# Image tower on one core: GpSimd's bulk work in the layers moved to the patch stage, ScalarE and PE

## The chip, the core and the metric

One Trainium2 chip, one of its cores. The metric is the device time of one launch in microseconds, median over runs. The engines are PE (TensorE, matmuls; its clock is granted at 1.2 or 2.4 GHz, shown as 0.50 and 1.00), VectorE (DVE), ScalarE (ACT), GpSimd (POOL) and SyncE (SP), which here issues every DMA. Everything is float32.

## What is computed

64 images of 84 x 84 pixels go through a tokenizer (patches of 14 x 14, windows of 3 x 3 patches with an attention inside each, one attention over the four windows of an image), which gives 6 tokens of 256 channels per image, 384 in all. Then come four residual steps, each after a layer norm:

```python
h = concat(cls_tok, L0_tok(x))
h = h + L0_attn(layernorm(h))   # gated scan along the tokens, then W_o and b_o
h = h + L0_ffn(layernorm(h))    # weight quantized to -1, 0, 1 times a scale
h = h + L1_attn(layernorm(h))   # 16 heads; output o_w and o_b
h = h + L1_ffn(layernorm(h))    # 8 experts, each with its top 48 tokens
```

Inside them, where the change touches them:

```python
# L0_attn(x): out = h_scan @ W_o.T + b_o
return x + out
# L1_attn: the head matrices
core_sym = 0.5 * (core + core.T)
centered = head_residual - head_residual.mean(axis=0, keepdims=True)
head_mats = core_sym[None] / float(H) + centered
...
y = y @ o_w.T + o_b
# L1_ffn(x): the normed tokens are a residual too
out = xf.at[flat_idx].add(o.reshape(k * n, d))
```

So the first and the fourth residual step add the normed tokens as well: h + norm(h) + product.

## The kernel before

The program is written engine by engine, each engine's queue in order, with semaphores between them. Three stages follow each other.

The patch stage has 19 tiles of 126 patches. For each, SP loads a tile into one of three buffers (L291), PE convolves it (L372), ScalarE copies it out (L1390), VectorE sums the windows (L870), takes statistics (L857, L879) and norms it (L864), GpSimd computes the reciprocal root of the variance (L1579, L1581) and keeps a copy of the normed tile (L1585), PE turns it. A norm of tile t - 1 stands behind the statistics of tile t. SP then loads the layer weights, with the head matrices at their end, in one DMA (L312). The window attention and the global attention follow.

In the layers the tokens lie as four tiles of 96 rows by 256 channels, in two groups (images 0 to 31 and 32 to 63) of two tiles. One norm is: VectorE's statistics (L1139, L1142), the reciprocal root on GpSimd (`rs_tokens`, L1569 and L1571, two small instructions), VectorE's norm of two tiles (L1153). PE turns the normed tiles (L644), ScalarE copies them (L1493), PE multiplies (`channels` L651, `tokens` L660).
GpSimd also does bulk work in the layers, in this order in its queue: behind the roots of the first norm, for each group, base = h + xn (L1648) and base + b_o (L1650); then the head matrices, 16 of 64 x 64, in nine instructions (L1664 to L1673), on which PE waits at L702; roots of the second norm; a memset (L1682); roots of the third norm; base = h + o_b (L1685); roots of the fourth and fifth norm; a memset (L1691); base = h + xn (L1695); the weighted picks (L1699). VectorE waits for `base_ready` before the first residual (L1203), the second norm (L1150), the third residual (L1289) and the output (L1375).

VectorE's gated scan: keep and gate from the tanh (L1183, L1184), gate times value (L1191), scan (L1194), for one group after the other, then the ternary weights (L1198 to L1201), then the first residual. In the last layer VectorE picks the top tokens in six rounds (L1312, L1317), with the fifth norm's two groups between them, while PE does 24 keep-warm matmuls (L749); the gather is L761.

## Time and profile before

| | us |
|---|---|
| median of 3 runs | 280.37 |
| lowest, highest | 278.83, 283.74 |
| the profiled execution | 281.46 |
| its span, first to last instruction | 279.7 |
| PE busy | 252.7 |
| VectorE busy | 154.4 |
| ScalarE busy | 66.8 |
| GpSimd busy | 67.9 |

The views of the trace are read like this. A time line has the start in us from the span's begin, the duration, the engine, the line, the operation, output and inputs with their shapes, and in brackets how long the engine was idle before and what ended it; rows of one line may be merged (x2: two instructions, from the start of the first to the end of the last). The chain of waits goes back from the last instruction to what released it, and is printed in order of time. A window row has the stretch, its length, the busy time and number of records for PE, PE's weight load, VectorE, ScalarE and GpSimd, the mean granted PE clock, the busy share of the DMA engines and GB/s. A group has the line, engine, operation and form with its count, then busy us, the mean in ns, and the idle time before.

### The profile page before, as it was taken

What the parts mean: (1) busy time and instruction counts of PE and PEld (TensorE: products, weight loads), DVE (VectorE), ACT (ScalarE), POOL (GpSimd) and SP (SyncE); (2) the same over time, 40 slices, a digit from 0 to 9 for tenths busy, and PEclk for the clock granted to TensorE, in tenths of its full rate; (3) what the DMA queues carried; (4) which work ended last, traced back from release to release, by engine and by line L of the source; (5) the groups of instructions that cost most, each with busy time, mean ns of one, the idle gap of its engine ahead of it and who ended that gap; (6) DMA issues with size and microseconds to landing.
All of it is one profiled execution on the core that took longest, in us unless ns stands there. A gap on an engine that the chain in (4) does not pass through costs nothing.

```text
span 279.7 us, 4102 instructions
## 1 busy us (share of the span) xinstructions
PE 252.7 (90%) x1467; PEld 194.5 (70%) x1467; DVE 154.4 (55%) x392; ACT 66.8 (24%) x166; POOL 67.9 (24%) x130
## 2 busy tenths in 40 slices
PE   6999999998999899789579899979989599999994
PEld 4888888975798677677457799856558454555562
DVE  1476767567685554459947444554358962621212
ACT  1134424235754422113010340000000003301200
POOL 0254434330222210199334100001017060000000
PEclk9999999999999887689989995555579979999999
DMA  6567754999400047980000000000000000676002
GB/s 196 160 223 225 223 177 117 415 404 428 187 1 2 0 111 243 425 348 2 0 1 0 2 0 2 0 0 0 0 0 4 1 0 0 231 294 227 2 0 56
DMA packets 8626, 32.94 MB, mean 118 GB/s; under 512 B 1056, under 2 KB 2848, under 8 KB 6432
## 3 DMA queue, kind: packets, MB, share of 16 engines
q1 hardware_dynamic: 8608, 32.70, 32.6%
q8 instruction: 11, 0.18, 0.3%
q14 instruction: 7, 0.06, 0.1%
HBM read 32.30 MB, written 0.39 MB: 117 GB/s over the span
## 4 chain that ended last, share of the span: by engine, by line
PE 70%; DVE 19%; issue 3%; ACT 2%; POOL 2%; DMA 1%; SPq 1%; DVEq 0%; POOLq 0%
PE bank L372 15%; PE bank L816 5%; PE bank L790 5%; PE bank L660 5%; DVE desk L1153 3%; PE bank L731 3%; PE bank L362 3%; PE bank L538 3%; PE bank L716 3%; PE bank L824 3%; PE bank L761 3%; PE bank L516 2%; PE bank L492 2%; PE bank L651 2%; PE bank L708 2%
## 5 line engine op out<-in xcount | busy, mean ns | idle before, releaser
L372 PE MATMUL bank<-desk,attic 118*126 118x256 f32 x190 | 43.9, 379 | 1.4 <-DMA desk<-conv_w 1.4
L362 PE MATMUL bank<-zeros 128*128 128x256 f32 x142 | 41.6, 442 | 1.1 <-POOL small L1562 1.1
L372 PEld LDWEIGHTS bank<-desk,attic 118*126 118x126 f32 x190 | 34.4, 188 | 6.2 <-DMA desk<-conv_w 1.8
L362 PEld LDWEIGHTS bank<-zeros 128*128 128x128 f32 x142 | 30.0, 221 | 7.0 <-issue 1.2
L1569 POOL TENSOR_SCALAR small<-small 96x2 f32<-96x2 f32 (+2 forms) x15 | 3.4, 226 | 87.5 <-DVE small L1142 77.7
L660 PE MATMUL bank<-layw,desk 128*96 128x256 f32 x48 | 16.7, 514 | 5.7 <-DVE desk L1194 3.6
L1493 ACT ACTIVATE desk<-bank 128x384 f32<-128x384 f32 x8 | 3.9, 491 | 62.3 <-PE bank L644 62.3
L660 PEld LDWEIGHTS bank<-layw,desk 128*96 128x96 f32 x48 | 10.1, 221 | 11.4 <-DVE desk L1194 4.2
L857 DVE BATCH_NORM_STATS2 small<-desk 126x6 f32<-126x256 f32 x19 | 8.1, 426 | 17.2 <-ACT desk L1390 17.1
L870 DVE TENSOR_REDUCE window_sums<-attic 118x70 f32<-118x630 f32 (+1 forms) x19 | 14.8, 784 | 4.3 <-DMA attic<-patches 3.8
L1390 ACT ACTIVATE desk<-bank 126x256 f32<-126x256 f32 x19 | 7.3, 384 | 40.3 <-PE bank L372 40.3
L1153 DVE TENSOR_SCALAR desk<-desk,small 96x256 f32<-96x256 f32 x20 | 13.4, 708 | 3.4 <-POOL small L1571 3.2
L1395 ACT ACTIVATE attic<-bank,cols 128x126 f32<-128x126 f32 (+1 forms) x38 | 14.9, 455 | 0.0
L731 PEld LDWEIGHTS bank<-desk,cons 48*128 48x128 f32 x48 | 11.4, 325 | 4.0 <-issue 2.7
L651 PE MATMUL bank<-desk,layw 128*128 128x192 f32 x72 | 13.3, 345 | 0.6 <-ACT desk L1493 0.6
L731 PE MATMUL bank<-desk,cons 48*128 48x32 f32 (+5 forms) x48 | 13.6, 455 | 0.0
L651 PEld LDWEIGHTS bank<-desk,layw 128*128 128x128 f32 x72 | 12.8, 205 | 0.9 <-ACT desk L1493 0.8
L1262 DVE TENSOR_TENSOR desk<-bank,desk 128x64 f32<-128x64 f32 (+5 forms) x12 | 4.7, 395 | 15.8 <-PE bank L731 12.5
L1579 POOL TENSOR_TENSOR small<-small 126x1 f32<-126x1 f32 x19 | 3.7, 193 | 37.6 <-DVE small L879 37.6
L516 PE MATMUL bank<-desk,attic 126*128 126x112 f32 (+1 forms) x76 | 10.5, 280 | 1.3 <-ACT attic L1438 0.7
L1346 DVE TENSOR_TENSOR desk<-bank,attic 128x512 f32<-128x512 f32 x8 | 5.5, 692 | 10.7 <-PE bank L790 10.7
L816 PE MATMUL bank<-resident_experts,desk 128*64 128x256 f32 x80 | 11.0, 382 | 0.5 <-DVE desk L1353 0.5
(189 smaller groups left out, 458.9 us busy)
## 6 DMA issues: line engine op xcount, KB each, us to landing
resident_experts<-experts SPq DMA_DIRECT2D x10, 1024.0 KB, 14.8
attic<-experts SPq DMA_DIRECT2D x6, 1024.0 KB, 10.3
attic<-patches SPq DMA_DIRECT2D x19, 315.0 KB, 2.9
layw<-layer_w SPq DMA_DIRECT2D x1, 2760.0 KB, 11.8
desk<-tokenizer_w SPq DMA_DIRECT2D x4, 576.0 KB, 4.5
attic<-bias SPq DMA_DIRECT2D x8, 256.0 KB, 4.5
cons<-constants SPq DMA_DIRECT2D x1, 692.0 KB, 5.5
desk<-conv_w SPq DMA_DIRECT2D x5, 128.0 KB, 3.1
```

The source lines that it names most:

```text
L362: mm(bank[b][:, 0:C], zeros[:, 0:P], zeros[:, :], start=True, stop=True)
L372: i = mm(conv_bank[j][0:TP, 0:C], xt[j][0:KP, k, :], convw[0:KP, k, :], start=(k == 0), stop=(k == KX - 1))
L516: i = mm(bank[4 + k][:, u * H8 * WT:u * H8 * WT + H8 * n], xhat_all[0:n * NWIN, t, k * P:(k + 1) * P], s_attT[q % RING][0:n * NWIN, u, 0:H ...
L538: i = mm(bank[b][:, m * width:(m + 1) * width], w_[:, k, m * P:(m + 1) * P], src[:, k, w * width:(w + 1) * width], start=(k == 0), stop=(k ...
L651: i = mm(bank[b][:, at:at + GT], w[:, k, cols_:cols_ + P], src[:, k, :], start=(k == 0), stop=(k == KC - 1))
L660: i = mm(bank[b][0:TR, u * C:(u + 1) * C], srcT[:, k, u * TR:(u + 1) * TR], w[:, k, :], start=(k == 0), stop=(k == KC - 1))
L731: i = mm(bank[4 * g + 1 + t % 3][:, p * GT:p * GT + GI * (t + 1)], spread[:, t, :], att[0][:, g * GI:(g + 1) * GI, p, 0:t + 1], start=True ...
L790: i = mm(bank[c][side * SW:(side + 1) * SW, :], ysT[:, k, e, :], w1[:, k, c * 512:(c + 1) * 512], start=(k == 0), stop=(k == KC - 1))
L816: i = mm(bank[4][side * SW:(side + 1) * SW, 0:C], hidT[q % 2][:, f, side * SW:(side + 1) * SW], w2[:, f, :], start=(f == 0), stop=(f == FC ...
L870: dve.tensor_reduce(sums[0:KP][:, bass.ds(t * (KX * WT), KX * WT)], xt[j][0:KP].rearrange("p k (w n) -> p (k w) n", n=NWIN), AX.X, ALU.add)\
L1153: ts(dst[0:TR, t, :], src[0:TR, t, :], t_mv[0:TR, t, 0:1], t_rs[0:TR, t:t + 1], ALU.subtract, ALU.mult).then_inc(s("xn_ready"), 1)
L1395: i = ac(winT[:, k, bass.ds(t * TP, TP)], tr_bank[j][:, k * P:k * P + TP], ACT.Identity, bias=col("kv_b", k), scale=col("kv_g", k))
```

## The change

- The weights of the heads move to the front of the packed layer weights and are loaded by a DMA of their own (64 rows, 4.5 KB each) behind the third patch tile's. The head matrices are made by GpSimd in the patch stage, one to three instructions in each of the tiles 3 to 12, in 13 instructions; the mean and the symmetric core are joined first, so one addition over four heads at a time is left. `tree` moves from the window sums to the token buffer h0T. GpSimd's loop over tiles 6 to 11 is written out.
- Residual plus norm is made by ScalarE for the first and the fourth norm, as h * (1 + r) - m * r with r the reciprocal root and m the mean: one activation for each tile (`with_norm`). GpSimd computes the two columns with three small instructions (`rs_and_shift`), one of them ahead of the root.
- The output biases b_o and o_b are put into the PSUM banks by PE, as a row of ones times the bias row (`bias_row`, two matmuls with one contraction row for each group), ahead of the token products. These take the place of `keep_warm(7, 3)` and `keep_warm(3, 1)`. The third residual then adds to h itself.
- Semaphores around the class query (`c_turned`, `c_q_done`, `c_qk_done`, `c_ln`, `c_qbd`) are joined into two. The waits stay where they were.

```diff
-LAYW, LAYW_N = offsets([("w_in", KC * 2 * C), ("w_s", KC * C), ("w_o", KC * C), ("tern", KC * C),
+LAYW, LAYW_N = offsets([("heads", NH * R), ("core", R), ("coreT", R), ("w_in", KC * 2 * C), ("w_s", KC * C), ("w_o", KC * C), ("tern", KC * C),
                         ("basis", KC * 2 * R), ("v_w", KC * C), ("o_w", KC * C), ("gate", KC * E8),
-                        ("heads", NH * R), ("core", R), ("coreT", R), ("bo_row", C), ("ob_row", C)])
+                        ("bo_row", C), ("ob_row", C)])
+HEADS_N = NH * R + 2 * R
...
+        tree = h0T[0:R].rearrange("p k i t -> p (k i t)")[:, 0:NH // 2 * R].rearrange("p (h r) -> p h r", r=R)
...
+        t_up, t_nm, t_dn, ones = tiny(TT), tiny(TT), tiny(TT), tiny(P, parts=1)
...
+            sp.dma_start(layw[0:R, 0:HEADS_N], layw_d[0:R, 0:HEADS_N]).then_inc(s("heads_in"), 16)
...
-            sp.dma_start(layw[:, :], layw_d).then_inc(s("layw_in"), 16)
+            sp.dma_start(layw[:, HEADS_N:], layw_d[:, HEADS_N:]).then_inc(s("layw_in"), 16)
...
-            def tokens(b, srcT, w, done):
+            def bias_row(b, name):
+
+                for u in range(TG):
+                    mm(bank[b][0:TR, u * C:(u + 1) * C], ones[0:1, 0:TR], w_of(layw, LAYW, name, parts=1),
+                       start=(u == 0), stop=False, skip_group_check=True)
+
+            def tokens(b, srcT, w, done, biased=False):
                 for u in range(TG):
                     for k in range(KC):
                         i = mm(bank[b][0:TR, u * C:(u + 1) * C], srcT[:, k, u * TR:(u + 1) * TR], w[:, k, :],
-                               start=(k == 0), stop=(k == KC - 1))
+                               start=(k == 0 and not biased), stop=(k == KC - 1), skip_group_check=biased)
...
-            keep_warm(7, 3)
+            pe.wait_ge(s("constants_set"), 4)
+            for g in groups:
+                bias_row(4 * g + 1, "bo_row")
             for g in groups:
                 pe.wait_ge(s("scan_ready"), g + 1)
-                tokens(4 * g + 1, scanT[:, g], lw["w_o"], "mix_done")
+                tokens(4 * g + 1, scanT[:, g], lw["w_o"], "mix_done", biased=True)
...
-            pe.wait_ge(s("heads_ready"), 1)
+            pe.wait_ge(s("heads_ready"), 4)
...
+                    bias_row(0, "ob_row")
                     pe.wait_ge(s("y_ready"), T - 1)
-                    tokens(0, yT[:, 0], lw["o_w"], "lat_out_done")
-            keep_warm(3, 1)
+                    tokens(0, yT[:, 0], lw["o_w"], "lat_out_done", biased=True)
+            bias_row(4, "ob_row")
             pe.wait_ge(s("y_ready"), (T - 1) * G)
-            tokens(4, yT[:, 1], lw["o_w"], "lat_out_done")
+            tokens(4, yT[:, 1], lw["o_w"], "lat_out_done", biased=True)
...
+                if n == 4:
+                    dve.wait_ge(s("shift_ready"), G + g + 1)
...
-                if n == 1:
-                    dve.wait_ge(s("base_ready"), g + 1)
...
-                dve.wait_ge(s("base_ready"), G + g + 1)
-                add_to_h(g, 4 * g, base, "lat_out_done", g + 1)
+                add_to_h(g, 4 * g, h, "lat_out_done", g + 1)
...
+            def with_norm(i, g):
+
+                act.wait_ge(s("up_ready"), G * i + g + 1)
+                act.wait_ge(s("shift_ready"), G * i + g + 1)
+                if i:
+                    act.wait_ge(s("h_ready"), 2 * G + g + 1)
+                for u in range(TG):
+                    t = TG * g + u
+                    n = ac(base[0:TR, t, :], h[0:TR, t, :], ACT.Identity, bias=t_dn[0:TR, t:t + 1],
+                           scale=t_up[0:TR, t:t + 1])
+                n.then_inc(s("base_ready"), 1)
+
+            for g in groups:
+                with_norm(0, g)
...
+                with_norm(1, g)
...
+            core = w_of(layw, LAYW, "core", parts=R)
+            coreT = w_of(layw, LAYW, "coreT", parts=R)
+            n_head = 0
+
+            def head_step(i):
+
+                nonlocal n_head
+                n_head += 1
+                i.then_inc(s("head_steps"), 1)
+                pool.wait_ge(s("head_steps"), n_head)
+
+            def prepare_heads(t):
+
+                if t == 3:
+                    pool.wait_ge(s("heads_in"), 16)
+                    head_step(pool.tensor_tensor(core, core, coreT, ALU.add))
+                    head_step(pool.tensor_scalar(core, core, 0.5 / NH, None, ALU.mult))
+                if t in (4, 5):
+                    a = 4 * (t - 4)
+                    head_step(pool.tensor_tensor(tree[:, a:a + 4, :], heads[:, a:a + 4, :], heads[:, a + 8:a + 12, :], ALU.add))
+                if t in (6, 7, 8):
+                    n = (4, 2, 1)[t - 6]
+                    head_step(pool.tensor_tensor(tree[:, 0:n, :], tree[:, 0:n, :], tree[:, n:2 * n, :], ALU.add))
+                if t == 8:
+                    head_step(pool.tensor_scalar(tree[:, 0, :], tree[:, 0, :], 1.0 / NH, None, ALU.mult))
+                    head_step(pool.tensor_tensor(core, core, tree[:, 0, :], ALU.subtract))
+                if 9 <= t < 13:
+                    four = heads[:, 4 * (t - 9):4 * (t - 8), :]
+                    pool.tensor_tensor(four, four, core.unsqueeze(1).to_broadcast([R, 4, R]), ALU.add)\
+                        .then_inc(s("heads_ready"), 1)
...
-            for t in range(HEAD):
+            for t in range(MID):
                 rs_tile(t, t % RING)
                 if t:
                     keep_xhat(t - 1, (t - 1) % RING)
                 if t == 3:
                     pool.wait_ge(s("c_norm"), 2)
                     rsqrt(c_ve[0:1], c_mv[0:1, 1:2], c_rs[0:1], "c_rs_ready", parts=1)
-            with pool.Fori(HEAD // RING, MID // RING) as r:
-                for j in range(RING):
-                    rs_tile(RING * r + j, j)
-                    keep_xhat(RING * r + (j - 1), (j - 1) % RING)
+                prepare_heads(t)
...
-            bo = w_of(layw, LAYW, "bo_row")[0:TR].unsqueeze(1).to_broadcast([TR, TG, C])
-            ob = w_of(layw, LAYW, "ob_row")[0:TR].unsqueeze(1).to_broadcast([TR, TG, C])
             groups = range(G)
-            part = lambda v, g: v[0:TR, TG * g:TG * (g + 1), :]
-
-            for g in groups:
-                rs_tokens(0, g)
-            for g in groups:
-                pool.wait_ge(s("xn_ready"), TG * (g + 1))
-                pool.wait_ge(s("h0_ready"), g + 1)
-                pool.tensor_tensor(part(base, g), part(h, g), part(xn, g), ALU.add).then_inc(s("base_step"), 1)
-                pool.wait_ge(s("base_step"), g + 1)
-                pool.tensor_tensor(part(base, g), part(base, g), bo, ALU.add).then_inc(s("base_ready"), 1)
-
-
-            pool.wait_ge(s("layw_in"), 16)
-            core = w_of(layw, LAYW, "core", parts=R)
-            coreT = w_of(layw, LAYW, "coreT", parts=R)
-            nh = 1
-
-            def hstep(i):
-                nonlocal nh
-                nh += 1
-                i.then_inc(s("head_steps"), 1)
-                pool.wait_ge(s("head_steps"), nh)
-
-            pool.tensor_tensor(core, core, coreT, ALU.add).then_inc(s("head_steps"), 1)
-            hstep(pool.tensor_tensor(tree, heads[:, 0:NH // 2, :], heads[:, NH // 2:NH, :], ALU.add))
-            n = NH // 4
-            while n:
-                hstep(pool.tensor_tensor(tree[:, 0:n, :], tree[:, 0:n, :], tree[:, n:2 * n, :], ALU.add))
-                n //= 2
-            hstep(pool.tensor_scalar(core, core, 0.5 / NH, None, ALU.mult))
-            hstep(pool.tensor_scalar(tree[:, 0, :], tree[:, 0, :], 1.0 / NH, None, ALU.mult))
-            hstep(pool.tensor_tensor(heads, heads, tree[:, 0:1, :].to_broadcast([R, NH, R]), ALU.subtract))
-            pool.tensor_tensor(heads, heads, core.unsqueeze(1).to_broadcast([R, NH, R]), ALU.add)\
-                .then_inc(s("heads_ready"), 1)
+
+            def rs_and_shift(n, g, i):
+
+                sl = slice(TG * g, TG * (g + 1))
+                pool.wait_ge(s("t_mv_ready"), TT * n + TG * (g + 1))
+                if i:
+                    pool.wait_ge(s("base_ready"), G)
+                pool.tensor_scalar(t_nm[0:TR, sl], t_mv[0:TR, sl, 0], -1.0, None, ALU.mult).then_inc(s("nm_ready"), 1)
+                rs_tokens(n, g)
+                pool.wait_ge(s("t_rs_ready"), G * n + g + 1)
+                pool.wait_ge(s("nm_ready"), G * i + g + 1)
+                pool.tensor_scalar(t_up[0:TR, sl], t_rs[0:TR, sl], 1.0, None, ALU.add).then_inc(s("up_ready"), 1)
+                pool.tensor_tensor(t_dn[0:TR, sl], t_nm[0:TR, sl], t_rs[0:TR, sl], ALU.mult)\
+                    .then_inc(s("shift_ready"), 1)
+
+            for g in groups:
+                rs_and_shift(0, g, 0)
...
-                pool.wait_ge(s("h_ready"), G + g + 1)
-                pool.tensor_tensor(part(base, g), part(h, g), ob, ALU.add).then_inc(s("base_ready"), 1)
-            for n in (3, 4):
-                for g in groups:
-                    rs_tokens(n, g)
+                rs_and_shift(3, g, 1)
+            for g in groups:
+                rs_tokens(4, g)
...
-            for g in groups:
-                pool.wait_ge(s("h_ready"), 2 * G + g + 1)
-                pool.wait_ge(s("xn_ready"), 3 * TT + TG * (g + 1))
-                pool.tensor_tensor(part(base, g), part(h, g), part(xn, g), ALU.add).then_inc(s("base_ready"), 1)
```

## Rows read from the trace of the kernel before

**Rows 1.** The page, busy time of each engine: us, share of span, instructions.
```profile
PE 252.7 (90%) x1467; PEld 194.5 (70%) x1467; DVE 154.4 (55%) x392; ACT 66.8 (24%) x166; POOL 67.9 (24%) x130
```

**Rows 2.** The chain of waits, 112 to 170 us: start, us, what.
```profile
119.89 2.69 DVE desk L1153 x2
...
130.19 2.65 DVE desk L1191
...
132.87 2.98 DVE desk L1194
...
138.99 0.68 DVE desk L1160
...
152.37 2.64 DVE desk L1153 x2
...
155.05 0.55 PE bank L644 x4
```

**Rows 3.** Time line of GpSimd (POOL) in the layers: start, us, instruction.
```profile
129.59 2.82 POOL L1672 TENSOR_TENSOR layw<-layw,window_sums 64x1024 f32<-64x1024 f32 x1
132.50 2.53 POOL L1673 TENSOR_TENSOR layw<-layw 64x1024 f32<-64x1024 f32 x1
...
152.30 2.54 POOL L1685 TENSOR_TENSOR desk<-desk,layw 96x512 f32<-96x512 f32 x2
...
212.16 2.64 POOL L1695 TENSOR_TENSOR desk<-desk 96x512 f32<-96x512 f32 x2
```

**Rows 4.** Time line of VectorE (DVE), same shapes, and norms at 212.91.
```profile
128.73 0.56 DVE L1191 TENSOR_TENSOR desk<-desk 128x384 f32<-128x384 f32 x1
129.32 0.96 DVE L1194 TENSOR_TENSOR_SCAN desk<-desk 128x384 f32<-128x384 f32 x1
...
207.62 0.73 DVE L1153 TENSOR_SCALAR desk<-desk,small 96x256 f32<-96x256 f32 x2 [1.13 <-POOL small L1571]
...
212.91 2.04 DVE L1153 TENSOR_SCALAR desk<-desk,small 96x256 f32<-96x256 f32 x2
```

**Rows 5.** Time line of PE; in brackets the idle time before.
```profile
118.29 3.75 PE L651 MATMUL bank<-desk,layw 128*128 128x192 f32 x16
...
123.76 5.47 PE L651 MATMUL bank<-desk,layw 128*128 128x192 f32 x32 [0.58 <-ACT desk L1493]
...
130.36 1.95 PE L660 MATMUL bank<-layw,desk 128*96 128x256 f32 x8
...
149.25 4.05 PE L362 MATMUL bank<-zeros 128*128 128x256 f32 x18
...
164.85 7.93 PE L716 MATMUL bank<-desk 128*48 128x12 f32 x128
...
183.41 3.73 PE L660 MATMUL bank<-layw,desk 128*96 128x256 f32 x8 [1.72 <-DVE desk L1270]
...
200.97 3.73 PE L660 MATMUL bank<-layw,desk 128*96 128x256 f32 x8 [0.41 <-DVE desk L1270]
...
225.85 7.09 PE L761 MATMUL bank<-desk 96*128 96x384 f32 x16
```

**Rows 6.** Windows: stretch, length, busy us of each engine, PE clock, DMA.
```profile
144.20:147.50 3.30, 3.30 (x10) 2.16 (x9) 0.00 (x0) 0.49 (x1) 0.00 (x0) 0.50 0.00 0
168.20:205.50 37.30, 35.18 (x145) 26.19 (x144) 16.70 (x42) 1.54 (x3) 0.92 (x2) 0.50 0.00 0
187.20:200.90 13.70, 13.36 (x38) 8.75 (x38) 6.13 (x18) 0.49 (x1) 0.92 (x2) 0.50 0.00 0
226.20:229.40 3.20, 3.20 (x6) 1.69 (x5) 3.00 (x3) 0.00 (x0) 3.20 (x3) 0.50 0.00 0
```

**Rows 7.** Windows, forty microseconds of the patch stage.
```profile
20.00:60.00 40.00, 40.00 (x234) 35.36 (x232) 25.85 (x67) 14.34 (x41) 15.60 (x43) 1.00 0.70 244
```

**Rows 8.** Groups by line and form, GpSimd: busy us, mean ns, idle.
```profile
L1569 POOL TENSOR_SCALAR small<-small 96x2 f32<-96x2 f32 x10 | 2.3, 228 | 77.7 <-DVE small L1142 77.7
...
L1668 POOL TENSOR_TENSOR window_sums<-window_sums 64x256 f32<-64x256 f32 x1 | 0.7, 724 | 0.1
```

28 lines of the change are left out of this document (14 added, 14 removed).

## The prediction

> **What bounds the kernel now.** I read the page's engine shares first, then the chain of waits, then the time lines of GpSimd, VectorE and PE over the layers, then the granted clock. The shares say that PE is busy 90% of the span and GpSimd 24% [rows 1], so GpSimd looks harmless. The chain says otherwise. Between 119 and 155 us it runs through four VectorE entries of 2.64 to 2.98 us: two pairs of norms (L1153), a multiplication (L1191) and a scan (L1194) [rows 2]. The GpSimd time line shows what stands beside them: the last two head instructions from 129.59 and 132.50, the bias additions from 152.30, and later residual plus norm from 212.16 [rows 3]. The reader is to see when the VectorE entries end. L1191 started 0.6 us after L1672 and ended 0.4 us after it; L1194 started 0.4 us after L1673 and ended 0.8 us after it [rows 2, 3]. The same shapes without a long GpSimd instruction beside them took 0.56 us, 0.96 us, and 0.73 us for a pair of norms [rows 4]. So in this trace such a VectorE instruction does not run slowly beside GpSimd, it waits for it. What the change removes is GpSimd's effect on VectorE, not GpSimd's own time.
>
> PE is the other bound: in the layers it works without a pause through its products [rows 5], at a granted clock of 0.50 (1.2 GHz) in several stretches, one of them 37.3 us long [rows 6]. In the patch stage PE is busy 40.00 of 40 us at 1.00 (2.4 GHz), while VectorE has 25.85 and GpSimd 15.60 [rows 7].
>
> **The change, part by part.** All sums are made in the profiled execution, which took 281.46 us, with a span of 279.7; the median of the three runs shown is 280.37, 1.1 lower.
>
> *First norm, GpSimd's four additions gone.* The pair from 119.89 would take 0.73 instead of 2.69 us [rows 2, 4]. GpSimd's new negated mean stands ahead of the reciprocal root: one more small instruction, 0.23 us [rows 8] and a gap, 0.3 together. The norms would end at 120.9 instead of 122.58. But PE is busy with the first group's products until 118.29 + 3.75 = 122.04 [rows 5] and turns the second group only then: **0.6** saved. With PE done earlier (part of that stretch ran at 1.2 GHz) it would be up to 1.7.
>
> *Gates and scan, head preparation gone.* The second group's L1191 and L1194 fill 130.19 to 135.85, 5.66 us [rows 2]. The first group's pair spans 128.73 to 130.28, 1.55 us [rows 4]. **4.1** saved. L1183 and L1184 ahead of them may have been held up too, but L1191 waits for ScalarE's tanh anyway; nothing counted.
>
> *Output bias by PE, first layer.* Four matmuls, eight records in the trace, replace six keep-warm records. Eight records of that width take 1.95 us [rows 5]. PE's products end at 123.76 + 5.47 - 0.6 = 128.6, the bias at 130.6, and two token products of 1.95 at 134.5. VectorE could do the second residual at 138.99 - 4.7 = 134.3 [rows 2]. So PE is late by **0.2**, a loss. VectorE's ternary weights lie under this. ScalarE's four activations for residual plus norm wait behind its last tanh. No row shows this form; 0.4 us each is an estimate from the norm of the same size on VectorE, 0.37. They end near 131, before VectorE overwrites h at 132.5, and ScalarE's next work, the copy of the turned second norm, comes 7 us later. Cost nothing; with that cover gone 1.5 us. The wait of VectorE's second norm on GpSimd's base goes, without effect.
>
> *Third norm, second bias addition gone.* The pair from 152.37 took 2.64 and would take 0.73, and the second group's turn follows it at 155.05 [rows 2]. PE is in keep-warm matmuls until 149.25 + 4.05 = 153.3 [rows 5] and turns the first group for about 0.4 after that. So the turn moves to 153.7: **1.35** saved, not 1.9.
>
> *Second bias by PE.* At 1.2 GHz a record of this width takes 3.73 / 8 = 0.47 us, so a bias row of four records takes 1.87. For the first image group it fills an idle 1.72 us (loss 0.15). For the second it replaces two keep-warm records (0.93 more) ahead of an idle 0.41 [rows 5] (loss 0.4 to 0.5). **0.55** lost; at 2.4 GHz nothing.
>
> *Last residual plus norm to ScalarE.* The norms from 212.91 took 2.04 behind L1695 and would take 0.73 [rows 3, 4]. They stand between two top-k steps on VectorE, and PE has only keep-warm matmuls (L749) until those are done, so it counts in full: **1.3** saved. ScalarE has nothing else there until the gather.
>
> *New small GpSimd work in the fourth norm.* The negated mean puts 0.3 on the chain. The two instructions behind the root, 0.23 us each by the form of L1569 [rows 8], start as VectorE's norm does and can hold it up by 0 to 0.5; I take 0.2. **0.5** lost. The same two in the first norm lie under PE's products. VectorE's new wait for them ahead of its fifth statistics (behind it stand the top-k steps) falls a norm later; they are done.
>
> *Head preparation in the patch stage.* Thirteen instructions over ten tiles, the longest ones 64x256; that shape took 0.72 us [rows 8]. By the share of [rows 7] GpSimd is free 61% of the time and VectorE 35%. At PE's pace of 2.4 us a tile that is 1.4 and 0.8 us. A head step can hold up VectorE's norm of a patch tile by up to 0.7, inside the 0.8 but nearly all of it. I take 0; the other end is 0.3 for each of ten tiles, 3 us. SP gets one more issue ahead of the load of tile 3, which waits for the first convolution anyway. GpSimd's wait for it stands at tile 3, with all later reciprocal roots behind; the data have some 10 us. The later weight load is smaller by as much.
>
> The Trainium skill, "SBUF — State Buffer", section "SBUF: two separate sides", speaks against this part: the shared port pair is held for a full instruction and the loser fully blocks. By that rule the head steps block VectorE wherever they stand, and moving them saves only where VectorE has slack. The sum by its worst case would be 3 us poorer, the end that I keep.
>
> *Clock.* PE's idle time between 130.36 + 1.95 = 132.3 and the scan's end at 135.85 goes away [rows 2, 5]. The fall to 0.50 at 144.2 came a few us after it, behind short turns and waits for the norms, and covered 3.3 us of the ternary products [rows 6]. At full clock these would take half; with the edges I count **1.2**. The wait ahead of the slots gets 1.3 shorter; the fall at 226 came after it. Six of 16 gather records started in 3.2 us at 0.50 [rows 6]; the other ten took 3.9 [rows 5], 0.39 each, so the six would take 2.3: **0.9**. Both are estimates, 0 to 1.6 each.
>
> **Sum.** 0.6 + 4.1 - 0.2 + 1.35 - 0.55 + 1.3 - 0.5 = 6.1 us without the clock, 8.2 with it. 281.46 - 8.2 = 273.3. The median run lies 1.1 lower, perhaps by the very stretches that I take off, so I subtract little of it: **273.0 us**.
>
> **Rivals.**
> *A. The clock rises in the long slow stretch.* It fell in the score matmuls of 12 columns, and 3.73 us of full products from 183.41 did not raise it [rows 5, 6]. Now the bias row stands right ahead of them, 5.6 us without a gap. If it rises there, VectorE sets the pace: from 187.2 to 200.9 it was busy 6.13 of 13.70 us [rows 6], so up to 7 go, and 1.8 of the next product; less some waiting, about 6.5 beyond my sum: 266.5 us. Against it: the bias rows feed one row of the array, and PE was busy 35.18 of the 37.30 us at 0.50 without a rise, much of it in matmuls with 48 rows. Chance 0.15. The Trainium skill, "TensorE: Matmul & The Clock Gate", Part 1, has the gate go by how busy PE is; by that rule a bias row counts like any matmul, which speaks for this rival, while the 35.18 us speak against the rule.
> *B. The patch stage pays.* The head steps hold up VectorE's norms beyond its slack, and PE, which has none, waits 3 us: 276.0. For it: the exact waiting in [rows 2, 3]. Against: the 0.8 us a tile. Chance 0.17.
> *C. Slower.* One-row matmuls in place of keep-warm ones let the clock fall in the first layer, and it stays down as it did from 168. Of the 20.7 us between the slow stretches 4.05 are keep-warm [rows 5, 6]; the rest at half clock costs up to 16.6 more: 281.5 - 6.1 + 16.6 = 292. It decides once more than 6 us of full-clock PE work run at half clock. Against it: 3.9 us of full products follow at once. Chance 0.04.
> *D. It doesn't do what it says.* The long instructions were late for another cause, or the wait moves to ScalarE's base: about 280. The ends in [rows 2, 3] speak against it. Chance 0.04.
>
> **How the numbers follow.** The forecast has 0.60, with its own range 270.5 to 275.5 (clock terms 0 to 2.8, first norm up to 1.1 more, the small holds). Range for 8 in 10: 267.0 to 277.0, which takes in B and leaves out C, D and the far side of A. The line at 2%, about what a measurement of this kernel can tell from no change, is 274.8. Faster: most of the forecast (0.54), A (0.15), a little of B (0.03): 0.72. Same: 0.24. Slower: 0.04.
>
> **What would show it.** Right: L1191 and L1194 of the second group near 0.5 and 1.0 us, all norm pairs near 0.7, the scan done near 131, the patch stage ending when it does now, the clock at 1.00 in the ternary products and the gather. Wrong: PE idle in the patch stage for L864 or GpSimd; ScalarE's new activations on the chain; the clock at 0.50 before 160. It fails most likely by the clock, which is given in long stretches, one of them worth as much as the whole change.

## The result, and the profile after

| | before | after |
|---|---|---|
| median, us (executions) | 281.37 (4) | 269.01 (4) |
| lowest, highest | 278.83, 283.74 | 266.22, 271.20 |
| ratio, 95% interval | | 0.9531, 0.9413 to 0.9649 |
| the profiled execution, its span | 281.46, 279.7 | 270.76, 269.0 |

The forecast was 273.0 us, range 267.0 to 277.0, chance of faster 0.72. The kernel is faster, inside the range, 4.0 us under the number forecast. Both kernels ran again in the three series below. Over all of them the kernel before has 31 executions from 272.0 to 284.2 us (median 278.5, mean 278.5) and the changed one 14 from 265.9 to 271.2 (median 268.9, mean 268.6): 9.9 us apart, with 1.8 us either side as a 95% interval from the two spreads. The interval in the table goes only by executions within 1.5% of each kernel's fastest, which later leaves out part of the kernel before's own spread, so the comparisons below are of medians over all executions.

The page of the changed kernel; [rows 1] answers to it.
```profile
PE 253.5 (94%) x1475; PEld 195.0 (72%) x1475; DVE 144.4 (54%) x392; ACT 70.6 (26%) x174; POOL 58.0 (22%) x139
```
The time line of VectorE, changed kernel: start, us, engine, line, instruction, idle before. L1164 is the norm, L1202 and L1205 the multiplication and the scan.
```profile
121.78 0.73 DVE L1164 TENSOR_SCALAR desk<-desk,small 96x256 f32<-96x256 f32 x2 [1.44 <-POOL small L1599]
...
131.49 0.53 DVE L1202 TENSOR_TENSOR desk<-desk 128x384 f32<-128x384 f32 x1
132.06 0.96 DVE L1205 TENSOR_TENSOR_SCAN desk<-desk 128x384 f32<-128x384 f32 x1
...
147.84 0.73 DVE L1164 TENSOR_SCALAR desk<-desk,small 96x256 f32<-96x256 f32 x2 [0.60 <-POOL small L1599]
...
204.08 0.71 DVE L1164 TENSOR_SCALAR desk<-desk,small 96x256 f32<-96x256 f32 x2
```
Against [rows 2, 4] the reader sees the same four places: 2.69 became 0.73, 2.65 and 2.98 became 0.53 and 0.96, 2.64 became 0.73, 2.04 became 0.71. The time line of PE, changed kernel (L661 the bias row, L668 the token products, L726 the scores, L364 keep-warm):
```profile
119.89 4.24 PE L653 MATMUL bank<-desk,layw 128*128 128x192 f32 x16
...
130.44 1.96 PE L661 MATMUL bank<-layw,small 1*96 1x256 f32 x8
...
141.27 3.62 PE L668 MATMUL bank<-layw,desk 128*96 128x256 f32 x16
...
159.18 6.81 PE L726 MATMUL bank<-desk 128*48 128x12 f32 x128
165.91 2.93 PE L364 MATMUL bank<-zeros 128*128 128x256 f32 x6
...
174.83 2.02 PE L661 MATMUL bank<-layw,small 1*96 1x256 f32 x4
176.78 3.73 PE L668 MATMUL bank<-layw,desk 128*96 128x256 f32 x8
...
215.73 6.73 PE L772 MATMUL bank<-desk 96*128 96x384 f32 x16
```
And its windows over the slow stretch, which [rows 6] shows as one of 37.3 us (stretch, length, busy us of PE, weight load, VectorE, ScalarE, GpSimd, PE clock, DMA):
```profile
163.50:181.00 17.50, 17.50 (x81) 13.46 (x80) 8.97 (x21) 1.04 (x2) 0.00 (x0) 0.51 0.00 1
184.00:198.00 14.00, 14.00 (x38) 9.18 (x37) 5.13 (x14) 0.49 (x1) 1.49 (x5) 0.51 0.00 0
```
Between the two stretches the clock was at 1.00 for 3 us. How far the changed kernel is ahead grows from place to place like this (us in either profile; negative is earlier):

| place | before | after | difference |
|---|---|---|---|
| first window scores | 65.91 | 67.74 | +1.8 |
| second turn of the first norm | 122.63 | 124.13 | +1.5 |
| end of the second scan | 135.85 | 133.02 | -2.8 |
| end of the ternary products | 149.42 | 144.89 | -4.5 |
| products behind the third norm | 155.60 | 149.68 | -5.9 |
| token products, first group | 183.41 | 176.78 | -6.6 |
| their end, second group | 204.70 | 195.64 | -9.1 |
| slots turned | 224.12 | 213.96 | -10.2 |
| end | 279.7 | 269.0 | -10.7 |

The first line is no part of the change: the changed kernel repeated has its window scores at 65.99 and 66.07. The 1.8 us are lost in PE's first convolutions, before and after:
```profile
6.47 6.74 PE L372 MATMUL bank<-desk,attic 118*126 118x256 f32 x30 [1.41 <-DMA desk<-conv_w]
```
```profile
6.33 8.66 PE L374 MATMUL bank<-desk,attic 118*126 118x256 f32 x30 [0.59 <-DMA desk<-conv_w]
```
They started no later, so the load of their weights is not the cause; the clock is shown as 1.00 in both, and no row says what it is. So the changed parts gained 12.5 us in this pair of profiles.

### The profile page after: what moved, and what is told of

Its sections match the earlier page's. It is cut to its first block, busy times and chain, and to the rows that moved or that the text cites. A ratio compares the mean times of both kernels' runs of the same rounds, so it can differ in the third digit from the quotient of the medians.

```text
span 269.0 us, 4125 instructions
## 1 busy us (share of the span) xinstructions
PE 253.5 (94%) x1475; PEld 195.0 (72%) x1475; DVE 144.4 (54%) x392; ACT 70.6 (26%) x174; POOL 58.0 (22%) x139
## 4 chain that ended last, share of the span: by engine, by line
PE 79%; DVE 12%; ACT 3%; issue 2%; POOL 2%; DMA 1%; SPq 1%; DVEq 0%; POOLq 0%
PE bank L374 16%; PE bank L827 5%; PE bank L801 5%; PE bank L364 5%; PE bank L653 5%; PE bank L741 4%; PE bank L668 4%; PE bank L540 3%; PE bank L835 3%; PE bank L726 3%; PE bank L518 2%; PE bank L494 2%; PE bank L772 2%; PE bank L718 2%; PE bank L436 2%
## 5 line engine op out<-in xcount | busy, mean ns | idle before, releaser
L374 PE MATMUL bank<-desk,attic 118*126 118x256 f32 x190 | 45.9, 392 | 0.6 <-DMA desk<-conv_w 0.6
L364 PE MATMUL bank<-zeros 128*128 128x256 f32 x134 | 39.8, 449 | 1.1 <-POOL small L1588 1.1
L374 PEld LDWEIGHTS bank<-desk,attic 118*126 118x126 f32 x190 | 35.7, 195 | 6.2 <-DMA desk<-conv_w 1.3
L364 PEld LDWEIGHTS bank<-zeros 128*128 128x128 f32 x134 | 28.9, 225 | 6.6 <-POOL small L1588 1.1
L1405 ACT ACTIVATE attic<-bank,cols 128x126 f32<-128x126 f32 (+1 forms) x38 | 14.9, 456 | 0.0
L668 PE MATMUL bank<-layw,desk 128*96 128x256 f32 x48 | 14.8, 470 | 0.0
L668 PEld LDWEIGHTS bank<-layw,desk 128*96 128x96 f32 x48 | 9.2, 201 | 5.0 <-DVE desk L1281 1.4
L741 PEld LDWEIGHTS bank<-desk,cons 48*128 48x128 f32 x48 | 10.0, 286 | 3.3 <-issue 3.0
L741 PE MATMUL bank<-desk,cons 48*128 48x32 f32 (+5 forms) x48 | 11.9, 413 | 0.0
L518 PE MATMUL bank<-desk,attic 126*128 126x112 f32 (+1 forms) x76 | 10.4, 278 | 1.3 <-ACT attic L1448 0.7
L1356 DVE TENSOR_TENSOR desk<-bank,attic 128x512 f32<-128x512 f32 x8 | 5.5, 692 | 10.7 <-PE bank L801 10.7
L801 PE MATMUL bank<-resident_experts,desk 128*64 128x512 f32 x40 | 11.0, 599 | 0.0
L1599 POOL TENSOR_TENSOR small<-small 96x2 f32<-96x2 f32 (+2 forms) x15 | 10.7, 712 | 1.3
## 6 DMA issues: line engine op xcount, KB each, us to landing
layw<-layer_w SPq DMA_DIRECT2D x1, 2184.0 KB, 10.4
```

Source lines behind the costliest of these rows:

```text
L364: mm(bank[b][:, 0:C], zeros[:, 0:P], zeros[:, :], start=True, stop=True)
L374: i = mm(conv_bank[j][0:TP, 0:C], xt[j][0:KP, k, :], convw[0:KP, k, :], start=(k == 0), stop=(k == KX - 1))
L518: i = mm(bank[4 + k][:, u * H8 * WT:u * H8 * WT + H8 * n], xhat_all[0:n * NWIN, t, k * P:(k + 1) * P], s_attT[q % RING][0:n * NWIN, u, 0:H ...
L668: i = mm(bank[b][0:TR, u * C:(u + 1) * C], srcT[:, k, u * TR:(u + 1) * TR], w[:, k, :], start=(k == 0 and not biased), stop=(k == KC - 1), ...
L741: i = mm(bank[4 * g + 1 + t % 3][:, p * GT:p * GT + GI * (t + 1)], spread[:, t, :], att[0][:, g * GI:(g + 1) * GI, p, 0:t + 1], start=True ...
L801: i = mm(bank[c][side * SW:(side + 1) * SW, :], ysT[:, k, e, :], w1[:, k, c * 512:(c + 1) * 512], start=(k == 0), stop=(k == KC - 1))
```

## Experiments

The kernels are the changed one with one edit, unless said otherwise. The median of the kernel before was 278.5 us in the first series (7 executions), 275.7 in the second (8), 276.4 in the third (12).

### First series: parts put back, the bias row, no heads

**e1_heads_back.** The head matrices are made behind the first norm again.
```diff
-                prepare_heads(t)
+            pool.wait_ge(s("heads_in"), 16)
+            head_step(pool.tensor_tensor(core, core, coreT, ALU.add))
...
+            pool.tensor_tensor(heads, heads, core.unsqueeze(1).to_broadcast([R, NH, R]), ALU.add)\
+                .then_inc(s("heads_ready"), 1)
```

> The changed kernel with the head matrices prepared by GpSimd in the layers again, behind the first norm, in nine instructions; everything else as changed. Waiting theory (VectorE's multiplication and scan wait until a long GpSimd instruction ends): the preparation starts near 122.5 us of the changed kernel's execution and its last two instructions run near 127 to 132.5, so the gates and the first multiplication are held to about 132.5 and the second scan ends 2 to 3 us later than now (near 135.5 instead of 133.0); 2 to 3 us slower than the changed kernel (269.0), and the ternary products may meet the clock at 0.50 again, up to 1.7 more: 271 to 274. Rival (the instructions were long for another cause, most of the gain is the clock): the scan ends as in the changed kernel, the time stays within 1 us of it.

Median 273.7 us (269.7 to 277.5). Time lines of GpSimd and VectorE of this kernel (L1194 and L1195 make keep and gate here, as L1183 and L1184 do in the kernel before), and the first group's token products on PE:
```profile
126.38 2.35 POOL L1719 TENSOR_TENSOR layw<-layw,h0T 64x1024 f32<-64x1024 f32 x1
128.81 2.34 POOL L1720 TENSOR_TENSOR layw<-layw 64x1024 f32<-64x1024 f32 x1
```
```profile
127.08 1.87 DVE L1194 TENSOR_SCALAR desk<-desk 128x384 f32<-128x384 f32 x1
128.87 2.50 DVE L1195 TENSOR_SCALAR desk<-desk 128x384 f32<-128x384 f32 x1
131.37 0.31 DVE L1194 TENSOR_SCALAR desk<-desk 128x384 f32<-128x384 f32 x1
```
```profile
180.06 3.73 PE L668 MATMUL bank<-layw,desk 128*96 128x256 f32 x8 [1.84 <-DVE desk L1281]
```
Now L1194 and L1195 are held (0.35 us each without), and the scan is not. L1194 ends 0.2 us behind L1719, L1195 0.2 us behind L1720. Counted from the first window scores, the scan ends 67.3 us behind, not 65.3: 2.05 us late. Which instruction is hit goes by what GpSimd does at that moment, and a fall of the clock at 132.5 appears behind it.

**e2_base_back.** Residual plus norm is GpSimd's again, in both layers; biases and heads stay as changed.
```diff
-            for g in groups:
-                with_norm(1, g)
...
+                pool.tensor_tensor(part(base, g), part(h, g), part(xn, g), ALU.add).then_inc(s("base_ready"), 1)
```

> The changed kernel with residual plus norm made by GpSimd again for the first and the fourth norm (base = h + xn, one instruction of 96x512 for each group, no three small instructions); biases by PE and heads as changed. Waiting theory: the pair of norms at 119.9 goes from 0.73 to about 2 us but lies under PE's products; the pair between the top-k steps goes from 0.71 to 2.0 (1.3 lost); the root of the fourth norm comes 0.3 earlier (gained). Sum 1.0 to 1.6 slower than the changed kernel: 270 to 270.6. Rival (ScalarE's path costs nothing and gains nothing): no difference beyond 0.5.

Median 272.1 us (265.0 to 274.1), a spread in which a part of 1 us can't be seen. Time lines of GpSimd and VectorE between the top-k steps:
```profile
196.25 2.64 POOL L1733 TENSOR_TENSOR desk<-desk 96x512 f32<-96x512 f32 x2
```
```profile
197.00 2.03 DVE L1164 TENSOR_SCALAR desk<-desk,small 96x256 f32<-96x256 f32 x2
```
From the end of the second token products to the slots it takes 19.4 us here and 18.3 in the changed kernel: 1.0, which is the 1.3 of the pair less the 0.3 of the negated mean. In the first norm the pair took 1.67, and the scan's end did not move (65.0 us behind the window scores, 65.0 in the repeated changed kernel). What the changed part saves there is nothing.

**e3_bias_128_rows.** The bias row is contracted over 128 rows, with ones of 1/128 (the bias stands in every row already).
```diff
-                    mm(bank[b][0:TR, u * C:(u + 1) * C], ones[0:1, 0:TR], w_of(layw, LAYW, name, parts=1),
+                    mm(bank[b][0:TR, u * C:(u + 1) * C], ones[:, 0:TR], w_of(layw, LAYW, name),
```

> The changed kernel with the bias row made from 128 contraction rows (1/128 times the bias, which is stored 128 times) in place of one; the same number of matmuls of the same width. If a matmul with one row does less than a full one to hold or raise the clock, the clock is raised in the long slow stretch (0.50 from 164 to 198 us in the changed kernel) and the kernel gains 2 to 6 us: 263 to 267, granted clock above 0.93. If rows don't matter to the clock: the same records of the same length, 269 within 1.5 us, mean clock 0.91 to 0.93.

Median 266.2 us (262.9 to 269.9). Time line of PE and a window of this kernel:
```profile
174.72 2.02 PE L661 MATMUL bank<-layw,small 128*96 128x256 f32 x4
176.53 2.37 PE L668 MATMUL bank<-layw,desk 128*96 128x256 f32 x8
```
```profile
163.50:177.50 14.00, 14.00 (x71) 11.43 (x70) 8.31 (x20) 1.04 (x2) 0.00 (x0) 0.51 0.01 1
177.50:194.50 17.00, 14.69 (x75) 9.98 (x74) 10.43 (x32) 1.03 (x3) 3.50 (x12) 1.00 0.00 0
```
This profile is a close pair with that of the changed kernel: the clock fell at 163.5 in both, and the bias rows began at 174.72 and 174.83. With one row the clock rose at 181.0 and fell again at 184; with 128 it rose at 177.5 and stayed until 194.5. The matmuls cost the same (2.02 us). It is one profile of each, and the four executions spread over 7 us, so the median doesn't settle it.

**e4_no_heads.** No head matrices are made at all, so the third residual step works with the raw head weights, which is another result.
```diff
-                prepare_heads(t)
...
-            pe.wait_ge(s("heads_ready"), 4)
+            pe.wait_ge(s("heads_in"), 16)
```

> The changed kernel without the preparation of the head matrices: they are used as loaded, so the fourth residual step is computed with other head matrices. It shows what the preparation costs in the patch stage. My account (hidden by VectorE's slack): within 0.5 us of the changed kernel, first scores of the window attention at the same distance from the first tile. Rival B of the prediction (the patch stage pays): about 3 us faster, 266.

Median 269.6 us (266.2 to 271.2), that of the changed kernel. Windows of the patch stage, this kernel and then the changed one repeated:
```profile
20.00:60.00 40.00, 40.00 (x235) 35.45 (x233) 25.99 (x67) 14.18 (x40) 15.82 (x43) 1.00 0.69 242
```
```profile
20.00:60.00 40.00, 40.00 (x234) 35.40 (x233) 26.29 (x67) 14.23 (x40) 22.20 (x56) 1.00 0.70 244
```
The 6.4 us of head work cost VectorE 0.3 us and PE nothing. In the changed kernel's first profile one of the 19 norms (L875) took 0.79 us instead of 0.41. It started beside a head step and ended 0.15 us behind it, and PE kept its pace:
```profile
22.96 0.72 POOL L1634 TENSOR_TENSOR h0T<-layw 64x256 f32<-64x256 f32 x1
```
```profile
23.04 0.79 DVE L875 TENSOR_SCALAR desk<-desk,small 126x256 f32<-126x256 f32 x1
```
Rival B falls.

### Second series: the heads alone, and the keep-warm matmuls

**f0_after_again.** The changed kernel, unedited.

> The changed kernel again, beside the variants. The sum of the prediction without the clock (6.1 us) puts it near 272.4 against the 278.5 that the kernel before had in the last series; the result on record says 269.0. Theory 1 (waiting behind GpSimd plus the clock): the gain beyond 6.1 us is clock, so profiles of this kernel whose stretches at 0.50 differ will differ by what those stretches hold, and the parts in the first layer will not: scan end minus start of the window scores 65.3 +- 0.3 us, third norm pair 0.73. Theory 2 (the gain beyond the sum is another effect of GpSimd, not the clock): spans agree within 1 us whatever the mean clock.

Median 267.7 us (265.9 to 271.0), spans 264.1 to 269.2. The profile (264.3) has the clock at 0.50 from 161.0 to 178.5 and then at 1.00 up to 209. Its scan ends 65.0 us behind the window scores, 65.3 on record. The first theory of the two holds: the parts agree, the executions differ by the clock.

**f5_heads_alone.** The kernel before, with only the head matrices moved to the patch stage.
```diff
+            sp.dma_start(layw[0:R, 0:HEADS_N], layw_d[0:R, 0:HEADS_N]).then_inc(s("heads_in"), 16)
...
+                prepare_heads(t)
...
-            hstep(pool.tensor_tensor(heads, heads, tree[:, 0:1, :].to_broadcast([R, NH, R]), ALU.subtract))
```

> The kernel before with one part of the change alone: the head matrices made in the patch stage; base additions, output biases and keep-warm stay as before. Theory 1 (VectorE waits for the long GpSimd instructions): the second group's L1191 and L1194 take 0.56 and 0.96 and the scan ends 4.1 us earlier (66.0 us behind the start of the window scores, not 69.9); PE's idle time there goes, so the clock does not fall at 144 (1.2 more); the pairs of norms stay at 2.6 to 2.7. Near 5.3 us faster than before at equal clock in the slow stretch. Theory 2 (in the layers the heads were hidden, the gain of the first layer comes with the base additions): the scan end moves by under 1 us. Theory 3 (the patch stage pays): the start of the window scores is 3 us later than 65.9 or 67.7.

Median 278.0 us (270.1 to 279.2), no gain that can be seen beside 275.7. Time lines of VectorE and GpSimd:
```profile
131.84 0.53 DVE L1192 TENSOR_TENSOR desk<-desk 128x384 f32<-128x384 f32 x1
132.41 0.96 DVE L1195 TENSOR_TENSOR_SCAN desk<-desk 128x384 f32<-128x384 f32 x1
...
148.18 2.62 DVE L1154 TENSOR_SCALAR desk<-desk,small 96x256 f32<-96x256 f32 x2 [0.60 <-POOL small L1572]
```
```profile
148.12 2.54 POOL L1692 TENSOR_TENSOR desk<-desk,layw 96x512 f32<-96x512 f32 x2
```
The scan ends 65.6 us behind the window scores, 69.9 in the kernel before: 4.3 us, and the clock does not fall at 144. The norm pair whose GpSimd addition stayed is still held, to the same end (150.80 and 150.66). At the start of the scores the kernel is 6 us earlier than before by the same count (92.9 against 98.9), and yet its executions have spans of 275.3, 277.4, 277.0 and 268.3. Its profile has the clock at 0.50 from 163.5 to 201.5, as long as the 37.3 us of the kernel before in [rows 6], and beside that one it is 4.4 us shorter (275.3 and 279.7). Three of its four executions have a mean clock of 0.889 to 0.901. Of the kernel before in this series spans were 271.5 to 282.1, and four of eight have 0.917 to 0.925. At like clock (0.936 and 0.925; 0.889 and 0.885) the heads alone are 3 to 5 us faster. So a part worth some 5 us is hidden in the medians, by how many executions of each kernel met the slow clock.

**f7_no_warm_after_scores.** Without the three keep-warm matmuls behind the scores.
```diff
-            keep_warm(3, 3)
```

> The changed kernel without the three keep-warm matmuls behind the scores of 12 columns. They took 2.93 us at 0.50 while the probabilities of the first image group were ready 2.5 us before they ended. Theory A (at 0.50 they are only in the way): the spread products start 2.5 us earlier, the clock rises no later, 2 to 2.5 us faster than the changed kernel. Theory B (they are what brings the clock back 12 us later, since PE is idle for lack of them): the rise comes at the end of the second group's token products or not at all, and the 0.50 stretch costs 3 to 6 us more: 0 to 3 us slower.

Median 266.5 us (265.1 to 268.0), 1.2 below the changed kernel in the same series, which this spread cannot tell from nothing. The clock rose at 178.0, so theory B is wrong. The spread products came 8.3 us behind the scores' start and not 10.0 as in f0_after_again; the scores themselves took 8.36 us since the clock fell 2.7 us into them.

**f8_warm_between_scores.** The same, with four keep-warm matmuls among the second group's scores.
```diff
+                    if g == 1 and i_ % 8 == 3:
+                        keep_warm(3, 1)
...
-            keep_warm(3, 3)
```

> The changed kernel with four keep-warm matmuls strewn among the second group's scores in place of the three behind them. The first group's scores, on which VectorE waits, are untouched. Theory A (the clock falls because the 12-column scores leave PE with little work for 6.8 us): with 1.8 us of full products among them it does not fall at 163.5, or rises sooner, and of the 17 us at 0.50 that follow up to 6 are saved. Theory B (the fall comes 4 us behind the scores' start and is settled by the first group's part): it falls at 163.5 as before, the four matmuls take about 3 us, and the time is that of the changed kernel within 1 us.

Median 274.1 us (269.4 to 275.5): 6.4 slower than the changed kernel, against both theories. Time line of PE (first the first of the four) and one window:
```profile
161.41 1.22 PE L364 MATMUL bank<-zeros 128*128 128x256 f32 x2
...
176.99 2.02 PE L661 MATMUL bank<-layw,small 1*96 1x256 f32 x4
178.93 3.73 PE L668 MATMUL bank<-layw,desk 128*96 128x256 f32 x8
```
```profile
161.00:202.50 41.50, 41.50 (x163) 29.36 (x162) 17.94 (x46) 1.53 (x3) 1.66 (x6) 0.51 0.00 1
```
The clock fell within the half microsecond from 161.0 on, and the first of the four matmuls started at 161.41, so they could hardly avert the fall; what the profile shows is that they did not end the stretch. And although a bias row stands ahead of the token products without a gap, as in the changed kernel, the clock did not rise: PE was busy 41.50 of 41.50 us and stayed at 0.50. So a row in front is not enough to lift the clock.

### Third series: the moment, a longer block, a dose

**g0_after_third.** The changed kernel again.

> The changed kernel once more, the neighbour of the three others in this series. Its profiles so far: the clock at 0.50 for 17.5 us from the scores of 12 columns on, then a rise at the end of the first group's token products, behind which it stayed up once (span 264.3 us) and fell again for 14 us once (269.0). Expected 264 to 270 us of span in every execution and none above 272, while the kernel before also has executions near 280.

Median 268.9 us (266.0 to 270.7), spans 264.1 to 268.9; the kernel before 270.2 to 282.4.

**g1_before_no_warm_after_scores.** The kernel before, without its three keep-warm matmuls behind the scores.
```diff
-            keep_warm(3, 3)
```

> The kernel before without the three keep-warm matmuls behind the scores (2.93 us at 0.50). Theory P (it is the moment at which full products meet the slow clock that decides on the rise, not the bias rows): the first group's token products start 12.9 us behind the fall instead of 15.4, near the 13.3 to 14.2 us of the profiles in which the clock rose there, so a share of the executions has the rise that the profile of before lacks; with the 2.5 us of keep-warm gone, 272 us or less in the median. Theory B (the bias rows in front of them are what lifts it, since they close the idle 1.7 us): no rise at that place, the stretch at 0.50 is again over 35 us long, and only 2.5 us are saved.

Median 275.6 us (268.4 to 281.2), 0.8 below the kernel before. The profiled execution was the slowest, with a span of 279.3: token products at 181.38, 12.4 us behind the fall at 169.0, and no rise until 203.5. Another execution had 266.6 us at a mean clock of 0.949, less than any of the 31 of the kernel before. Neither forecast came: theory P had 272 us or less, theory B 2.5 us saved. But without any bias row an execution can be far better; which place of the trace made it so was not profiled.

**g3_dense_block.** No keep-warm behind the scores, bias rows with 128 rows, and the second group's bias row right behind the first group's token products.
```diff
-            keep_warm(3, 3)
...
+                    pe.wait_ge(s("att_probs"), 2)
+                    bias_row(4, "ob_row")
-            bias_row(4, "ob_row")
```

> The changed kernel with three edits: no keep-warm behind the scores, the bias rows with 128 contraction rows, and the second group's bias row right behind the first group's token products, so that 7.7 us (at 0.50) of products with 128 rows or 96 columns of output stand without a gap. Theory P (a longer block of full products meets the moment wherever it lies): the clock rises inside or at the end of this block in every execution, the second bias costs nothing at the end; spans 259 to 263 us, 3 to 6 us under the changed kernel. Theory R (the rise depends on something else): the spread is that of the changed kernel without keep-warm, 263 to 266 us, with executions that stay at 0.50 near 270.

Median **261.5 us** (260.1 to 264.9, 6 executions), 7.5 under the changed kernel and 14.9 under the one before in the same series. The means differ from the changed kernel's by 6.9 us, plus or minus 2.3. Time line of PE and two windows:
```profile
170.58 2.02 PE L661 MATMUL bank<-layw,small 128*96 128x256 f32 x4
172.39 3.58 PE L668 MATMUL bank<-layw,desk 128*96 128x256 f32 x8
175.80 1.03 PE L661 MATMUL bank<-layw,small 128*96 128x256 f32 x4
```
```profile
162.00:176.00 14.00, 13.64 (x66) 11.18 (x65) 8.66 (x21) 1.04 (x2) 0.00 (x0) 0.51 0.01 1
176.00:186.00 10.00, 8.44 (x44) 5.74 (x43) 6.05 (x18) 0.49 (x1) 1.55 (x5) 1.00 0.00 0
```
The clock rose inside the block, at 176.0, and the second bias row ran behind the rise in 1.03 us instead of 2.02. Five of six spans lie between 258.3 and 260.0. This version beats both kernels. It is more than either theory had (3 to 6 us). Two of its three edits had been tried alone in earlier series (e3_bias_128_rows 266.2, f7_no_warm_after_scores 266.5); the moved bias row was not, and nothing takes the three apart within one series.

**f6_dose_third_norm.** Two additions on GpSimd put back beside the third norm, into a tile that nobody reads, with waits that keep the order.
```diff
+                pool.tensor_tensor(part(base, g), part(h, g), part(h, g), ALU.add).then_inc(s("head_steps"), 1)
```

> The changed kernel with two additions of 96x512 on GpSimd put back beside the third norm, into a tile that nobody reads (h plus h). Theory 1 (a VectorE norm that starts beside a long GpSimd instruction ends with it, and PE's keep-warm matmuls cover part of that): the pair of norms takes 2.5 to 2.7 us instead of 0.73, the following products start 1.35 us later, not 1.9 (83.3 us behind the start of the window scores instead of 81.9). Theory 2 (GpSimd's additions were harmless, the gain there had another source): the pair stays at 0.73 and the products where they are.

One execution, 266.7 us. GpSimd, VectorE and a row of the chain of waits:
```profile
142.10 2.08 POOL L1726 TENSOR_TENSOR desk<-desk 96x512 f32<-96x512 f32 x2
```
```profile
142.17 2.16 DVE L1164 TENSOR_SCALAR desk<-desk,small 96x256 f32<-96x256 f32 x2 [0.60 <-POOL small L1600]
```
```profile
144.94 3.93 PE bank L653 x24
```
The additions took 2.08 us, with one tile as both operands, not 2.54, and the pair of norms 2.16: it ended 0.15 us behind them. The following products start 17.6 us behind the scan's end instead of 16.7, so of 1.43 us of waiting 0.9 arrive. The expectation had 1.35 later, for a pair of 2.5 to 2.7 us. The count from the window scores that was expected is useless here: the clock did not fall at 107 to 123 in this execution, and the scan ended after 61.5 us, 3.8 sooner than in the changed kernel on record.

## Why the prediction was right

The direction rested on one reading, that VectorE's long instructions wait for GpSimd's and end with them. The two kernels with heads moved or put back, the one with the base put back and the dose all show it, and rival D (another cause) falls with them.

- *Gates and scan*: forecast 4.1, measured 4.3, in the changed kernel and with the heads alone. L1183 and L1184 (L1194 and L1195 after the change), for which nothing was counted, went from up to 0.95 us to 0.35.
- *First norm*: forecast 0.6 (0.6 to 1.7), measured 0.3 or nothing. The step that failed is the 122.04 at which PE was to be done. The first group's products took 4.24 us instead of 3.75, since the clock was at 0.50 for the first 3.0 us of them, not for 1.9.
- *Output bias*: a loss of 0.2 was forecast; the tokens began at 132.34 and the second residual came 2.8 us earlier, as the scan did. No loss.
- *Third norm*: forecast 1.35, measured 1.4. PE's keep-warm matmuls covered the rest, and the dose repeats it: 1.43 put in, 0.9 out.
- *Second bias*: forecast 0.55 at 1.2 GHz. The first group's part cost 0.2; the second's cannot be told from the clock around it.
- *Last residual plus norm, small GpSimd work*: forecast 1.3 gained and 0.5 lost. 1.3 came; of the 0.5, the 0.3 of the negated mean is real and the hold-up of 0.2 was not there.
- *Patch stage*: forecast 0, and measured 0 in e4_no_heads. Rival B, at 0.17, had the waiting right but not VectorE's slack. For the rule of the Trainium skill, "SBUF — State Buffer", section "SBUF: two separate sides", the trace agrees that a full instruction is waited out (the 0.79 us for 0.41 above). That this costs nothing where VectorE has slack is what e4_no_heads shows. The worst case of 3 us was not reached.
- *Clock*: this term was mis-sized. The ternary products gave 1.7 us (forecast 1.2), the gather 0.4 (0.9). For the gather the forecast had the clock fall go with the shorter wait for the slots; that wait went from 3.21 to 1.88 us, and the clock still fell, at 215.0, and stayed at 0.50 until 218.5, 2.8 us into the gather. The long stretch, counted at nothing, gave 3.4: the token products of the first group came 1.0 us earlier against the scores' start, and the way from them to the end of the second group's went from 21.3 us to 18.9, with the second group's bias row in it. That is half of rival A, whose 6.5 us needed a clock that stays up, as f0_after_again has it (span 264.3).

So 7 of the 12.5 us are the waits, near the forecast (6.1), and 5.5 are the clock against the 2.1 forecast. The sum had no step for the 3.4 us; that they came, and no more of them, is luck. Rival C did not come: the clock was at 1.00 from 123 to 163.5. The profiled execution began 1.8 us late, which hid part of it.

Rival A's reason does not stand. It named the bias row that closes the gap. f8_warm_between_scores has the row and no gap, and no rise; e1_heads_back has a gap of 1.84 us ahead of its token products and a rise at their end (184.0). What the profiles share is the time at which full products come after the fall. In six profiles (after, e2, e4, f0, f7, g0) the first group's token products began 13.1 to 14.3 us behind it (the fall read to half a microsecond), and the clock rose within 0.5 us of their end; with 128 rows in the bias (e3, g3) they began 13.0 and 10.4 us behind it, and it rose before their end. At 12.4 (g1) and at 15.4, 15.7 and 17.9 us (before, f5, f8) it did not, and the stretch lasted 34.5 to 41.5 us. The three keep-warm matmuls behind the scores are a like case: they raised the clock in e1_heads_back (at 174.0) and f6_dose_third_norm (166.5), where they began about 7 us behind the fall, and in none of the others that have them (2 to 5 us behind it). In those two the clock fell again, at 177.0 and 169.5, and rose at the end of token products that began only about 3 us behind that. So the same work raised the clock or not by when it came, but no single distance from the fall is the rule. That the change helped by bringing the products to a better moment, besides what it saved, fits the profiles and is not shown by a run that moves them alone. The Trainium skill, "TensorE: Matmul & The Clock Gate", Part 1, has the gate watch in a rhythm that is independent of the kernel, and different counts from run to run of one kernel; the spans of the kernel before, 270.2 to 282.4 us in one series, agree. It also has the clock go by how busy PE is. With busy read from the records that does not come out: 41.50 of 41.50 us at 0.50.

What stays open: whether a bias row over 128 contraction rows brings the clock back sooner than one over a single row in general (one pair of profiles says so), which of g3's three edits carries its gain, and why a start 12.4 us behind the fall brought no rise when 13.1 did, and 10.4 in g3: it was one profile. The three profiles of the changed kernel had the rise, and none of its 15 spans is over 269.4 us; that it always has it is not shown.

## What to carry to other kernels

Where a VectorE entry has several times the duration of the same shape elsewhere, look at which GpSimd instruction ends just before it; moving that to a stage where VectorE has slack gives back the whole wait, less what PE's fillers cover. Work out the waits and the clock separately, and compare parts from one anchor to the next within a profile, since a part worth 5 us can vanish in medians that one slow-clock stretch spreads over 10 us. Where PE comes out of many small matmuls, try its full products in one block without a gap rather than thin fillers between them; here that was the fastest version, though which of its edits did it is open.

## What the runs showed of the hardware

- VectorE waits with one SBUF input as well: TENSOR_SCALAR of 128x384 took 1.87 and 2.50 us beside 64x1024 additions on GpSimd, and 0.35 alone (e1_heads_back).
- Four keep-warm matmuls among 12-column scores, the first at 161.41 and so just behind the fall, did not bring the clock back; it stayed down for 41.5 us of work without a gap (f8_warm_between_scores).
- A bias row over 128 rows cost as much as over one (2.02 us at 0.50, 1.10 at 1.00), and in the one pair of profiles the clock rose 3.5 us sooner behind it.
- The gather's 16 records took 5.40 us (g3) to 8.78 us (f0, e4) in the same place of the program, by the clock alone.
- The first window scores came at 65.8 to 66.8 us or at 67.6 to 67.8, for kernels with the same start; the difference lies in the first 30 convolutions (8.66 us for 6.74 in the changed kernel and the one before), which started no later, and its cause is open.
